# Issue point of the copy of x to the output in a delta-rule, convolution and feed-forward block

## What is computed

```python
x = L0_attn_hidden_states
xn = _layernorm(x, axis=-1)
x = x + _L0_attn_ref(xn, ...) + _L0_ffn_ref(xn, ...)
```

```python
q, k, v = short_conv_silu(xn @ W, conv_w)        # causal, 4 taps, for each of q, k, v
beta = sigmoid(xn @ Wb)
delta_out = delta_rule_chunkwise(q, k, v, beta)  # inverts a unit lower triangular matrix per chunk
ms_out = multiscale_conv(v, w3, w15, w31) @ kernel_mix_w, then @ channel_mixer_w
gates = softmax(gelu(cat(xn, mean|ms_out|, mean|delta_out|, mean|v|) @ w1 + b1) @ w2 + b2)
o = gates . (ms_out, delta_out, v)
o = o * rsqrt(mean(o * o) + 1e-5) * o_norm_w
return o @ Wo
```

## Time and profile before

| | |
|---|---|
| device time, median of 3 runs | 3813.25 us (3811.24 to 3821.89) |
| device time of the profiled execution | 3814.92 us |
| its span, first to last instruction | 3813.1 us |
| TensorE busy | 3381.8 us, 89% |
| VectorE busy | 3159.1 us, 83% |
| ScalarE busy | 2760.3 us, 72% |
| GpSimd busy | 760.7 us, 20% |
| mean granted TensorE clock | 0.936 |

### The profile page before, as it was taken

The page is one execution under the profiler, slowest core; times in us unless marked ns, Lnnn a source line. Parts: engine busy times, 40 slices in busy tenths (PEclk is TensorE's granted clock), DMA queues, the critical chain, the costliest instruction groups (busy, mean ns, idle before and its releaser), DMA issues.

```text
span 3813.1 us, 69963 instructions
## 1 busy us (share of the span) xinstructions
PE 3381.8 (89%) x22848; PEld 2513.9 (66%) x22848; DVE 3159.1 (83%) x7856; ACT 2760.3 (72%) x9144; POOL 760.7 (20%) x1489
## 2 busy tenths in 40 slices
PE   6898889988889888889888898888898888988877
PEld 5666667666667666667666676666666666766654
DVE  5988889888789888798888898888988888888884
ACT  5676778766777667777767776677776777766774
POOL 2012221112221122211122211222112221112220
PEclk8999999999999999999999999999999999999988
DMA  6012211112211122211222111222112221112220
GB/s 176 13 37 47 47 41 36 27 37 47 47 35 35 24 47 47 42 31 25 42 47 47 35 35 24 47 47 42 32 21 46 47 47 32 34 28 47 41 40 7
DMA packets 188307, 154.92 MB, mean 41 GB/s; under 512 B 111804, under 2 KB 146108, under 8 KB 187688
## 3 DMA queue, kind: packets, MB, share of 16 engines
q0 software_dynamic: 31744, 79.70, 12.2%
q1 hardware_dynamic: 156200, 70.76, 7.1%
HBM read 51.34 MB, written 52.95 MB: 27 GB/s over the span
## 4 chain that ended last, share of the span: by engine, by line
PE 48%; ACT 23%; DMA 15%; issue 8%; DVE 4%; POOL 1%; ACTq 0%; POOLq 0%; DVEq 0%; SPq 0%
DMA my<-prod 14%; PE front L516 6%; PE dense L721 6%; PE dense L674 5%; PE dense L678 5%; PE dense L754 5%; PE dense L662 5%; ACT my L1106 3%; DVE my L1531 2%; PE cell L637 2%; PE small L690 2%; ACT dense L1136 2%; ACT prod L1117 2%; PE cell L644 2%; PE cell L645 1%
## 5 line engine op out<-in xcount | busy, mean ns | idle before, releaser
L1531 DVE SCALAR_TENSOR_TENSOR my<-vT,mw,my 128x256 f32<-128x256 f32 x5408 | 2233.9, 481 | 34.8 <-DMA my<-prod 20.2
L516 PE MATMUL front<-xsh,wk 128*128 128x256 f32 x1024 | 291.0, 448 | 252.7 <-ACT raw L894 252.7
L721 PE MATMUL dense<-xsh,w 128*128 128x256 f32 x2048 | 481.9, 381 | 4.0
L516 PEld LDWEIGHTS front<-xsh,wk 128*128 128x128 f32 x1024 | 232.4, 230 | 306.1 <-ACT raw L894 264.1
L1117 ACT ACTIVATE prod<-vT,mw 128x256 f32<-128x256 f32 x480 | 210.6, 509 | 295.5 <-DMA my<-prod 295.4
L397 POOL TENSOR_SCALAR vare<-xsq 128x2 f32<-128x2 f32 x32 | 6.2, 193 | 2096.8 <-ACT xsh L856 2096.8
L721 PEld LDWEIGHTS dense<-xsh,w 128*128 128x128 f32 x2048 | 368.4, 190 | 72.1 <-ACT xr L1168 11.1
L1507 DVE SCALAR_TENSOR_TENSOR xr<-xsh,rest,xr 128x256 f32<-128x256 f32 x128 | 53.7, 482 | 277.4 <-ACT xk L1072 277.4
L1079 ACT ACTIVATE ka<-dense 128x512 f32<-128x512 f32 x64 | 38.2, 597 | 314.7 <-PE dense L662 314.7
L457 POOL DMA_DIRECT2D my<-prod x160 | 146.4, 915 | 540.0 <-ACT prod L1117 341.0
L662 PE MATMUL dense<-xk,wfk 128*128 128x256 f32 x1024 | 236.8, 385 | 12.0 <-DVE xk L1507 10.1
(11 more groups left out here) (182 smaller groups left out, 7021.9 us busy)
## 6 DMA issues: line engine op xcount, KB each, us to landing
my<-prod POOLq DMA_DIRECT2D x160, 384.0 KB, 4.2
xa<-in_x SPq DMA_DIRECT2D x32, 512.0 KB, 4.5
rows_out<-Bm SPq DMA_DIRECT2D x64, 256.0 KB, 4.2
out<-xb POOLq DMA_DIRECT2D x32, 512.0 KB, 6.1
Yq<-units_out SPq DMA_DIRECT2D x128, 32.0 KB, 3.1
w<-in_w SPq DMA_DIRECT2D x1, 2048.0 KB, 16.5
Bu<-rows_out SPq DMA_DIRECT2D x32, 64.0 KB, 3.1
units_out<-Xu SPq DMA_DIRECT2D x32, 64.0 KB, 2.5
```

Source lines behind the costliest of these rows:

```text
L516: i = e.matmul(by_batch(front[pair % 2][:, c * W:(c + 1) * W]), wt[:, k, hs(c0 + c)], xsh[s % 2][:, k, :, 1:1 + P], start=(k == 0), stop=( ...
L721: e.matmul(by_batch(o), w1[:, k, hs(2 * pair + c)], xsh[s % 2][:, k, :, 1:1 + P], start=(k == 0), stop=False)
L1531: i = e.scalar_tensor_tensor(o, vT[s % 2][:, c, :, off:off + P], mw[:, col:col + 1], o, ALU.mult, ALU.add)
```

## The change

On SyncE, `copy_x(i - 1)` no longer stands between `load_x(i + 1)` and `write_units(i - 1)`. It stands behind `read_units(i - 1)`, as the last thing of the index.

```diff
                 if 1 <= i < NS - 1:
                     load_x(i + 1)
                 if 1 <= i <= NS:
-                    copy_x(i - 1)
                     write_units(i - 1)
                     read_units(i - 1)
+                    copy_x(i - 1)
```

## The result

The changed kernel takes 3518.64 us, median of 4 runs (3513.48 to 3537.3). The kernel before, on the same chip, takes 3814.49 us (3811.24 to 3821.89). The ratio is 0.923, with a 95% interval of 0.919 to 0.927: 296 us less, where 286 were forecast. The profiled execution of after has a span of 3517.3 us.

A forecast was written before the change was run, and what follows sets the result against it. No engine was full; ScalarE's wait for an add slowed by the copy stopped all four engines. 28 steps saving 9.7 us (272), 5 for an odd step and 9 at the ends made 286: 3527 us, range 3495 to 3612.

The forecast's parts named there:

- Add 3.0: Accumulating DMA of a tap product, beside the copy: to land in 5.1 us, not 15.7, removing ScalarE's 9.53 us wait.
- the sum: Forecast saving in an ordinary step: 9.7 us, between 9.2 and 10.4, taking it from 116.90 to 107.2 us.
- the range named: ScalarE's waits for `my<-prod` over the whole span were to fall from 295 to 20 to 50 us.
- the estimate of 10.8 us: Copy's 8 rows of 64 KB on two DMA engines, four behind one another at 2.7 us each.
- the 2.16 us: TensorE's gain in 16 projection matmuls if its clock stays at 2.4 GHz; 0.3 counted, bounds 0 and 1.0.
- Rival 5: Instruction loads behind 64 KB rows starve TensorE at the inverse's small matmuls, 2.7 us a step: 3605 us; chance 0.03.
- The new place: Copy issued with the four `Yq` reads: no cost taken for its own wait, add 3.3, those reads or `add_out`.
- Rival 2: Copy falls on add 3.3, VectorE waits 11.2 us, each step 1.5 us longer: about 3841 us; chance 0.05 in full.
- add 3.3: Add that VectorE needs before head 3's taps: to land in 4.2 us, 0.6 us behind the copy's issue, cost 0.
- One earlier packet of the copy: A copy packet ahead of add 3.3's completion costs 2.7 us a step, 76 in all: 3603 us; chance 0.03.
- Rival 1: GpSimd's inverse becomes the bound through a late read of `Bu`; steps of 110.0 us, 3608 in all; chance 0.07.
- The ends: Three steps at the program's ends, outside the 29 counted: 9 us saved, between 0 and 20.

The follow-up runs named there:

- Spread_old: Kernel before, with the copy of x left at its old place but cut into 16 parts (16 KB rows on 16 DMA engines): 3558.97 us, ratio 0.932.
- four_old: Kernel before, with the copy at its old place in 4 parts (two 64 KB rows on each of four DMA engines): 3684.81 us, ratio 0.965.
- between: Changed kernel, with the copy issued after the writing of the units but ahead of the reads of `Yq`: 3970.81 us, ratio 1.042 to the kernel before.
- spread_new: Changed kernel, with the copy at its new place cut into 16 parts: 3543.31 us, ratio 0.928 to the kernel before.
- no_copy: Changed kernel without the copy of x and the waits on it, so the output lacks x: 3526.44 us, ratio 0.923 to the kernel before.
- phase64: Changed kernel with 64 more transposes of the identity (128 instructions) at TensorE's start: 3521.3 us, ratio 0.925 to the kernel before.
- spread_between: Changed kernel, with the copy in 16 parts, between the writing and reading back of the units: 3658.45 us, ratio 0.958 to the kernel before.

## Why the prediction was right, and where it was not

**The cause and its price were right.** Add 3.0 landed in 5.1 us, as forecast. The time from the issue of `rows_out` to VectorE's transposition of `Yq` fell from 44.81 us to 35.00, by 9.81 where 9.7 was the sum; in the mean of the 18 ordinary steps it fell by 9.4. ScalarE's waits of 22.0 us lie in the range named, and the `wk` projections are as quick as those of `wv` (227.9 and 228.7 us in all). The mean clock of 0.980 stands at the edge of what was named, above 0.98. Spread_old and four_old show that it was the rows of 64 KB on two engines, which the prediction had only read from packets. It had named two pairs of packets, at 1936.5 and at 1942.0. The trace of before has four, begun at 1933.0, 1936.9, 1939.6 and 1942.3 us. The first pair takes 3.7 us and the others 2.4, as in the DMA view of before from 1942.2 to 1942.3 us, where two packets take 304% of 1.6 us:

```profile
q1 hardware_dynamic: 2, 0.13, 304.0%
```

So the estimate of 10.8 us for the four behind one another is near the 11.7 us from the first start to the last end. The Trainium skill (page "DMA: Bandwidth & Descriptors", section "Why a DMA increments its semaphore by 16 and not by 1") says that a DMA is split over as many engines, up to 16, as divide its slowest dimension that is not 1. By that rule the copy, whose slowest dimension is 2, is on two engines, and 16 parts put it on 16. The runs agree: in before its packets come in pairs.

**A second drop of TensorE's clock was not in the sum.** Of the 2.16 us that the `wk` projections gain I counted 0.3, and the runs leave room for little more: these matmuls lie ahead of the transposition of `Yq`, where the step fell by 9.4 to 9.8 us, and the wait alone was to give 9.4. But from the transposition of `Yq` to the next `rows_out`, where the sum had nothing, the step fell from 72.09 to 70.40 us. These are stretches of before: that part of step 15, the same part of the step shown (step 16), and a piece of the latter.

```profile
1852.99:1923.73 70.74, 68.34 (x561) 49.17 (x560) 64.19 (x167) 59.22 (x197) 3.64 (x6) 1.00 0.05 8
1968.54:2040.63 72.09, 69.62 (x561) 50.64 (x560) 64.38 (x168) 59.12 (x197) 3.65 (x6) 0.98 0.05 8
1986.50:1989.90 3.40, 3.21 (x15) 3.21 (x16) 2.67 (x7) 0.14 (x1) 0.00 (x0) 0.50 0.01 2
```

In the step shown the granted clock is 0.50 a second time, for 3.4 us, and line 630 runs through it. Its row before, and then after:

```profile
1986.69 2.07 PE L630 MATMUL cell<-S,kT 128*128 128x128 f32 x8 [0.67 <-ACT X L1032]
1831.88 1.16 PE L630 MATMUL cell<-S,kT 128*128 128x128 f32 x8 [0.67 <-ACT X L1032]
```

The clock records of before have this second drop, of 3.4 or 6.8 us, in 26 of the 29 steps. The three without it (4, 15 and 25) take 70.3 to 70.7 us for this part, as the ordinary steps of after do, the others 72.0 in the median. So the 1.7 us a step that the sum missed is the second drop. Why the clock fell there is not traced: TensorE waits 0.67 us ahead of line 630 before and after, and after it does not fall. Over all 29 steps the part up to `Yq` gave 263.3 us, where the sum had 277. The part behind it gave 16.2, where the sum had nothing, although the odd steps lose most of their time there.

**The odd steps were not in the sum.** They are most of the 46 us that are given back. Rival 5 named the starving of TensorE, with the right place (the small matmuls of the inverse) and the right size of one (0.2 to 2.2 us in after and up to 4.0 elsewhere, 2.7 named), but the wrong cause and count: five steps and not all, and without the copy as well. Its total of 78 us was too high, since it comes seldom. Its step was too low where the clock falls too. In step 15 the break is 0.8 us, but 16 matmuls behind it take 5.41 and not 3.72 us, a second low stretch of 3.4 us follows, and the step is 4.1 us longer. Why before had no break is not shown. That its engines stood still for 9 us is not enough: in between TensorE stands 11.4 to 12.2 us right ahead of these small matmuls and breaks off in all six steps.

**The new place was free, as said.** Reads of `Yq` ahead of the copy landed in 2.1 us, faster than before. Rival 2 did not come about: add 3.3 does not wait for the copy, since VectorE's longest wait for `my<-prod` is 2.3 us. Between shows that its price was right (15.0 us for the add) and that one place earlier it falls due. One earlier packet of the copy holding back add 3.3's completion would have cost 2.7 us a step, 76 in all. VectorE's waits for any add come to 24.3 us in the whole span, so the trace does not show it. In the ordinary step the case did not arise: add 3.3 was issued at 1806.93 and landed in 4.2 us, at 1811.1, and the copy's first packets start at 1812.6. The rule of the Trainium skill behind it (same page, section "Queues, rings and completion order"), that a completion lands only after every earlier write of its DMA engine from any queue, is therefore not tested there. Rival 1 did not come about: GpSimd waits 21.8 us for `Bu` in 32 steps, 2.2 at most, less than the 34.1 us of before, where the rival had every step 2.8 us longer.

**The ends.** The three outer steps gave 16.3 us, where I took 9 and allowed 0 to 20. I have not traced these.

**What stays open.** Why the packet comes later in spread_new and no_copy than in after, at the same edges (2.5 us of break in the mean against 1.0); why before and steps 7, 17 and 27 of phase64 have no break; why the clock fell a second time in before; why step 29 is longer; and rival 2 by itself, since in between and spread_between `Yq` is late as well.

## What to carry to other kernels

When a small transfer is late though the DMA engines are nearly empty, look for a neighbour that lies on few of them in long rows, and spread it, or move it to a place where nobody asks for a transfer while it runs (11 to 12 us here). In the same queue it must stand behind what is urgent. Price a wait that is removed together with the clock that comes back, and look through the whole step for stretches of low clock: here the one right behind the wait gave next to nothing, and a second one, 44 us behind the first, gave 1.7 us a step. And after a wait is gone, look at the few steps that did not get shorter before putting them down to the thing that was moved.

## What was not expected of the hardware

TensorE can run short of instructions in a dense stretch of small matmuls (64 matmuls in 0.7 us) for 0.2 to 4.0 us. In a given step it broke off behind the same matmul in every kernel, the steps in question moved by five when 128 instructions were put ahead, and it went on 0.8 to 1.6 us after a packet of instructions had ended. In after the four breaks of 0.6 to 2.2 us were followed by the lower clock, with 16 matmuls in 5.4 to 6.1 us where they take 3.7 at the higher one; the break of 0.2 us was not. And a copy of 512 KB in 8 rows of 64 KB held up an add beside it by 10 to 11 us (15.0 and 15.7 us to land, 4.2 to 5.1 without it), and the reads behind it in its own queue by 11 us, while one in 16 parts cost the add 1 to 2 us (6.3 us).
